# Group averages of channel statistics: a TensorE product against VectorE's 32-partition turns

## The reference

```python
# x (64, 256, 28, 28) f32; M (256, 256, 3, 3); Z (8, 256, 256, 3, 3); alpha (256, 1, 1); rv (1, 8)
def _gn(v, G=32, eps=1e-5):
    g = v.reshape(B_, G, C_ // G, H_, W_)
    m = jnp.mean(g, axis=(2, 3, 4), keepdims=True)
    s = jnp.var(g, axis=(2, 3, 4), keepdims=True)
    return ((g - m) / jnp.sqrt(s + eps)).reshape(v.shape)

A = m * m + jnp.sum(z * z, axis=0) / 100.0
w = (rv @ (z * lax.rsqrt(A)))[0] + m * lax.rsqrt(A)
out = conv3x3(jnp.sign(_gn(x)), jnp.sign(w), padding=1) * alpha
return x + out
```

## Time and profile before

| | us |
|---|---|
| median of 3 runs | 524.27 (523.59 to 525.61) |
| the profiled execution, its own time | 522.31 |
| its span (first to last instruction) | 520.5 |
| HBM read and written | 72.62 MB and 51.38 MB, 238 GB/s over the span |

### The profile page before, as it was taken

How to read it: one execution, slowest core, us unless ns; L and a number is a source line. 1 busy time by engine, 2 the same in 40 slices (tenths; PEclk the granted TensorE clock), 3 DMA queues, 4 the chain that set the end, 5 groups by cost and what they waited for, 6 DMA issues and landing times.

```text
span 520.5 us, 8289 instructions
## 1 busy us (share of the span) xinstructions
PE 482.7 (93%) x2794; PEld 401.2 (77%) x2794; DVE 375.4 (72%) x711; ACT 328.8 (63%) x566; POOL 22.8 (4%) x70
## 2 busy tenths in 40 slices
PE   0898969899999999999999999999999999999990
PEld 0454637788888888888888888888888888888880
DVE  1122458757977978878879879879779779776656
ACT  0787766577667667676676676676676766754320
POOL 8200000000000000000000000000000000000000
PEclk9999997989999999999999999999999999999996
DMA  6999958018568578568568568568577577544226
GB/s 235 399 396 396 397 216 345 0 63 309 214 220 307 191 243 276 211 243 290 191 242 287 195 241 295 191 241 292 197 251 273 210 261 268 202 148 186 87 100 247
DMA packets 45644, 124.37 MB, mean 239 GB/s; under 512 B 3632, under 2 KB 3632, under 8 KB 45616
## 3 DMA queue, kind: packets, MB, share of 16 engines
q1 hardware_dynamic: 45616, 124.01, 65.8%
HBM read 72.62 MB, written 51.38 MB: 238 GB/s over the span
## 4 chain that ended last, share of the span: by engine, by line
PE 86%; DVE 4%; DMA 3%; ACT 2%; SPq 2%; issue 2%; DVEq 0%; ACTq 0%
PE conv_ps L353 80%; DMA m_sb<-in_L_conv_M_dram 3%; SPq L245 2%; PE conv_ps L294 2%; ACT whole L409 1%; DVE x_sb L699 1%; PE conv_ps L307 1%; DVE bn L623 1%; PE conv_ps L297 1%; PE conv_ps L311 1%; PE grp_ps L337 1%; DVE low L605 0%; ACT signs L459 0%; DVE whole L673 0%; ACT low L414 0%
## 5 line engine op out<-in xcount | busy, mean ns | idle before, releaser
L353 PE MATMUL conv_ps<-signs,wts 128*128 128x492 f32 (+5 forms) x1926 | 425.5, 381 | 2.4 <-ACT signs L459 2.1
L353 PEld LDWEIGHTS conv_ps<-signs,wts 128*128 128x128 f32 x1926 | 361.6, 190 | 59.0 <-ACT signs L459 2.5
L467 ACT ACTIVATE part<-conv_ps 128x492 int32<-128x492 f32 (+3 forms) x107 | 61.4, 574 | 147.0 <-PE conv_ps L353 147.0
L459 ACT ACTIVATE signs<-x_sb,shift,rstd 128x784 fp32r<-128x784 f32 x128 | 125.8, 1035 | 0.8 <-DVE shift L660 0.8
L673 DVE SCALAR_TENSOR_TENSOR whole<-conv_ps,part 128x492 int32<-128x492 f32 (+3 forms) x107 | 70.9, 663 | 73.5 <-PE conv_ps L353 65.2
L681 DVE SCALAR_TENSOR_TENSOR low<-whole,conv_ps 128x492 f32<-128x492 int16 (+3 forms) x107 | 70.5, 659 | 3.7
L699 DVE SCALAR_TENSOR_TENSOR x_sb<-whole,alpha_sb,x_sb 128x784 f32<-128x784 int16 x64 | 66.0, 1031 | 0.7
L699 DVE SCALAR_TENSOR_TENSOR x_sb<-low,alpha_sb,x_sb 128x784 f32<-128x784 f32 x64 | 65.9, 1029 | 0.0
L642 DVE BATCH_NORM_STATS2 bn<-x_sb 128x6 f32<-128x392 f32 x116 | 59.7, 557 | 0.8 <-issue 0.6
L437 ACT ACTIVATE unread<-x_sb 128x784 bf16<-128x784 f32 x58 | 49.2, 848 | 0.0
L439 ACT ACTIVATE unread<-x_sb 128x784 bf16<-128x784 f32 x58 | 49.1, 847 | 0.0
(11 more groups left out here) (46 smaller groups left out, 150.5 us busy)
## 6 DMA issues: line engine op xcount, KB each, us to landing
x_sb<-in_x_dram SPq DMA_DIRECT2D x64, 784.0 KB, 5.7
out_dram<-x_sb SPq DMA_DIRECT2D x64, 784.0 KB, 3.8
x_sb<-in_L_conv_Z_dram SPq DMA_DIRECT2D x64, 288.0 KB, 7.4
m_sb<-in_L_conv_M_dram SPq DMA_DIRECT2D x8, 288.0 KB, 8.3
alpha_sb<-in_L_conv_alpha_dram SPq DMA_DIRECT2D x2, 0.5 KB, 2.4
rv_sb<-in_L_conv_rv_dram SPq DMA_DIRECT2D x1, 4.0 KB, 2.4
```

The costliest lines, as they stand in the source:

```text
L353: mm = pe.matmul(sums_of_tile(b, skip, drop), wts[:, ch, kh * KW + kw], e, start=n == 0, stop=n == PRODUCTS - 1, skip_group_check=True)
L459: nc.scalar.activation(o, x_sb[:, slot_of(t, j), h].rearrange("p (a b) -> p a b", b=W), ACT.Sign, bias=shift[:, t % BODY, j, h:h + 1], sca ...
L467: nc.scalar.activation(part[:, bank(b), 0:columns(b)], conv_ps[bank(b)][:, 0:columns(b)], ACT.Copy, scale=-FRACTION / PACK, bias=FRACTION ...
```

## The change

The matrix average, its PSUM bank grp_ps, the TensorE product of each group and ScalarE's copy of it go. VectorE makes the averages with four operations for each group: it turns the blocks of 32 partitions of chan over (32 columns now, of which the first 4 * images hold numbers, so that a partition holds one number and a column one channel), sums runs of CPG columns, multiplies by 1 / CPG, and turns the result back, each average read CPG times, into grp. Each of the four waits for the one before. chan and grp grow to 32 columns, and GpSimd sets chan to zero once in place of building the matrix. GpSimd's variance waits for the turn back.

In the list of VectorE the turn stands ahead of everything else of b = 0, the sum and the scaling behind everything of b = 0, and the turn back ahead of b = 1, in every triple, the first included. In the weight phase, group 0's turn stands behind sums_of_both(0), its other three operations one unit later behind unit_w, and all four of group 1 between copy_taps(3) and copy_taps(5).

```diff
-        average = sb("average", [P, P], F32)
...
-        chan = sb("chan", [P, BODY, TRI, 4], F32)
-        grp = sb("grp", [P, BODY, TRI, 4], F32)
+        chan = sb("chan", [P, BODY, BLOCK // 4, 4], F32)
+        grp = sb("grp", [P, BODY + 1, BLOCK // 4, 4], F32)
+        by_value = sb("by_value", [P, 2, BLOCK], F32)
+        group_sum = sb("group_sum", [P, 2, BLOCK // CPG], F32)
+        group_mean = sb("group_mean", [P, 2, BLOCK // CPG], F32)
...
-        grp_ps = psum("grp_ps", [P, 512], F32)
...
-            def group(g, t, j0, j1, images):
-
-                need(pe, act_sums_done, (images - EARLY) * 2)
-                pe.wait_ge(dve_sums_done, images)
-                need(pe, grp_copied, g)
-                pe.matmul(grp_ps[:, 0:4 * (j1 - j0)], average[:],
-                          chan[:, t % BODY, j0:j1].rearrange("p j k -> p (j k)"), start=True,
-                          stop=True).then_inc(grp_done, 1)
...
-                if c == UNITS - 4:
-                    group(0, 0, 0, 1, 1)
             unit_a(UNITS - 1)
             pack_taps(1)
-            group(1, 0, 1, TRI, TRI)
...
                         first_products(k, t, b, min(b + 1, TRI), number)
-                        if b == (3 if first and t == 0 else 0) and width(t + 1, last) > 0:
-                            group(k + 2, t + 1, 0, width(t + 1, last), k * TRI + TRI + width(t + 1, last))
...
-            def copy_group(g, t, j0, j1):
-                act.wait_ge(grp_done, g + 1)
-                nc.scalar.activation(grp[:, t % BODY, j0:j1].rearrange("p j k -> p (j k)"),
-                                     grp_ps[:, 0:4 * (j1 - j0)], ACT.Copy).then_inc(grp_copied, 1)
...
-                if c == UNITS - 3:
-                    copy_group(0, 0, 0, 1)
...
-            copy_group(1, 0, 1, TRI)
...
-                        if b == (3 if start else 0):
-                            copy_group(k + 2, t + 1, 0, then)
...
+            after(nc.gpsimd.memset(chan[:], 0.0))
...
-                pool.wait_ge(grp_copied, g + 1)
+                pool.wait_ge(grp_done, g + 1)
...
+            def group_turn(g, t, images):
+
+                need(dve, act_sums_done, (images - EARLY) * 2)
+                dve.wait_ge(dve_sums_done, images)
+                nc.vector.transpose(by_value[:, t % 2], chan[:, t % BODY].rearrange("p j k -> p (j k)")
+                                    ).then_inc(grp_step, 1)
+
+            def group_add(g, t):
+
+                dve.wait_ge(grp_step, g * 3 + 1)
+                nc.vector.reduce_sum(group_sum[:, t % 2], by_value[:, t % 2].rearrange("p (g c) -> p g c", c=CPG),
+                                     axis=mybir.AxisListType.X).then_inc(grp_step, 1)
+
+            def group_scale(g, t):
+
+                dve.wait_ge(grp_step, g * 3 + 2)
+                nc.vector.tensor_scalar(group_mean[:, t % 2], group_sum[:, t % 2], 1.0 / CPG, None,
+                                        ALU.mult).then_inc(grp_step, 1)
+
+            def group_back(g, t, spot=None):
+
+                spot = t % BODY if spot is None else spot
+                dve.wait_ge(grp_step, g * 3 + 3)
+                nc.vector.transpose(grp[:, spot].rearrange("p (g c) k -> p g (c k)", c=CPG // 4),
+                                    group_mean[:, t % 2].unsqueeze(2).to_broadcast([P, BLOCK // CPG, CPG])
+                                    ).then_inc(grp_done, 1)
...
                 if c == UNITS - 5:
                     sums_of_both(0)
+                    group_turn(0, 0, 1)
+                if c == UNITS - 4:
+                    group_add(0, 0)
+                    group_scale(0, 0)
+                    group_back(0, 0, BODY)
...
             copy_taps(3)
+            group_turn(1, 0, TRI)
+            group_add(1, 0)
+            group_scale(1, 0)
+            group_back(1, 0)
             copy_taps(5)
...
                     for b in range(TILES):
+                        if b == 0:
+                            group_turn(k + 2, t + 1, k * TRI + TRI + then)
+                        if b == 1:
+                            group_back(k + 2, t + 1)
                         if b >= 2 and b - 2 < later and b > 2:
...
                         if not start and 1 <= b < 1 + TRI:
                             outputs(t - 1, b - 1, end)
+                        if b == 0:
+                            group_add(k + 2, t + 1)
+                            group_scale(k + 2, t + 1)
```

More of the change, by code:

```diff
@@ L68, in conv_preact @@
     CPG = C // GROUPS
+    BLOCK = 32
+    assert BLOCK % CPG == 0 and TRI * 4 <= BLOCK
     INV_LAG = 2
@@ L74, in conv_preact @@
     KQ = P // QUAD
-    CONST_STEPS = 2 * 4 + 3 + 3 + 1 + KQ
+    CONST_STEPS = 2 * 4 + 3 + 1 + 1 + KQ
     Z_DMAS = 16 * (K // KQ * KQ + 1)
@@ L164, in conv_preact @@
         bn_step = sem("bn_step")
+        grp_step = sem("grp_step")
         grp_done = sem("grp_done")
-        grp_copied = sem("grp_copied")
         var_step = sem("var_step")
@@ L549, in _, with variance @@
                                               base=0, pattern=[[-1, P]], channel_multiplier=1))
[L550 to L556, removed]
+            after(nc.gpsimd.memset(chan[:], 0.0))
             nc.gpsimd.memset(signs[:].bitcast(F32), 0.0).then_inc(borders_zero, 1)
-            def variance(g, t, j0, j1):
-                pool.wait_ge(grp_copied, g + 1)
+            def variance(g, t, j0, j1, spot=None):
+                pool.wait_ge(grp_done, g + 1)
                 v = slice(j0, j1)
-                mean = grp[:, t % BODY, v, 0:4:2]
+                spot = t % BODY if spot is None else spot
+                mean = grp[:, spot, v, 0:4:2]
                 nc.gpsimd.tensor_tensor(mean_sq[:, t % BODY, v], mean, mean, ALU.mult).then_inc(var_step, 1)
                 pool.wait_ge(var_step, g * 2 + 1)
-                nc.gpsimd.tensor_tensor(var[:, t % BODY, v], grp[:, t % BODY, v, 1:4:2], mean_sq[:, t % BODY, v],
+                nc.gpsimd.tensor_tensor(var[:, t % BODY, v], grp[:, spot, v, 1:4:2], mean_sq[:, t % BODY, v],
                                         ALU.subtract).then_inc(var_step, 1)
-            variance(0, 0, 0, 1)
+            variance(0, 0, 0, 1, BODY)
             variance(1, 0, 1, TRI)
@@ L655, in bounded, with negative_mean @@
                                         ALU.add).then_inc(var_done, 1)
-            def negative_mean(g, t, j0, j1):
+            def group_turn(g, t, images):
[12 more added lines that the diff above has]
+            def group_back(g, t, spot=None):
+                spot = t % BODY if spot is None else spot
+                dve.wait_ge(grp_step, g * 3 + 3)
+                nc.vector.transpose(grp[:, spot].rearrange("p (g c) k -> p g (c k)", c=CPG // 4),
+                                    group_mean[:, t % 2].unsqueeze(2).to_broadcast([P, BLOCK // CPG, CPG])
+                                    ).then_inc(grp_done, 1)
+            def negative_mean(g, t, j0, j1, spot=None):
+                spot = t % BODY if spot is None else spot
                 dve.wait_ge(rstd_done, g + 1)
-                nc.vector.scalar_tensor_tensor(out=shift[:, t % BODY, j0:j1], in0=grp[:, t % BODY, j0:j1, 0:4:2],
+                nc.vector.scalar_tensor_tensor(out=shift[:, t % BODY, j0:j1], in0=grp[:, spot, j0:j1, 0:4:2],
                                                scalar=-1.0, in1=rstd[:, t % BODY, j0:j1], op0=ALU.mult,
@@ L709, in _ @@
                     sums_of_both(0)
+                    group_turn(0, 0, 1)
[3 more added lines that the diff above has]
+                    group_back(0, 0, BODY)
                 if c == UNITS - 2:
                     bounded(0, 0, 0, 1)
-                    negative_mean(0, 0, 0, 1)
+                    negative_mean(0, 0, 0, 1, BODY)
             unit_w(UNITS - 2)
```

## The result

| | before | changed |
|---|---|---|
| median of 6 runs, us | 524.36 (522.71 to 525.61) | 518.30 (517.04 to 519.63) |
| span of the profiled execution | 520.5 | 515.3 |
| step of a triple (90 products) | 19.79 | 19.57 |
| VectorE busy in a triple | 16.47 | 17.10 |

The ratio is 0.9887, 95% interval 0.9861 to 0.9913, so 4.6 to 7.3 us less, 5.9 in the middle. The forecast was 4.7 us less, 519.6 us.

A forecast was written before the change was run, and what follows sets the result against it. TensorE was taken to bound the kernel in the triples. Removing 21 group products gives -4.9 us, group 0 in the weight phase +0.25, so -4.7: 524.27 to 519.6 us, range 517.5 to 522.4.

The forecast's parts named there:

- The bound: In the triples TensorE alone bounds the kernel, busy all 19.80 us of one, with VectorE at 16.47 and ScalarE at 13.55.
- The price of a group, 0.235 us: On TensorE, the same pair of products with and without a group between: 0.65 against 0.42 us, unrounded 0.235.
- the chain's 0.12: Rival price of a group on TensorE: only 0.12 us for each of 21, time 522.0 us; chance 0.10 including a second variant.
- 21 groups: Of 23 groups 21 lie in the triples, all on the path, first triple included: 21 x 0.235 = 4.9 us less.
- The four operations, 0.91 us: Added to VectorE per group: three at 0.25 and one at 0.16 us, 1.07 us with waits; bounds 0.64 and 3.0.
- The cover in the triples: VectorE's added 1.07 us fits into 3.33 us of idle time per triple, slips have 10 us; price nothing.
- rival C: Every triple: VectorE becomes the bound from 3.33 us a group; at 4.1 us, 16 us more, 540; chance 0.05.
- Group 0, +0.25 us: Weight phase: the turn ahead of m_sq delays the path by 0.25 us, from 0.16 to 0.6 by the bounds.
- Group 1, hidden in 1.33 us: Weight phase: the four operations, 1.07 us, fit into VectorE's 1.33 us idle ahead of copy_taps(5), costing nothing.
- The first triple: VectorE reads the first tile up to 1 us later, covered by 10 us; TensorE's 2.07 us pause before 103.66 stays.
- The sum: Whole kernel: -4.9 + 0.25 = -4.7 us, from 524.27 to 519.6 us; forecast's chance 0.72.
- Rival B: TensorE's clock: one half-rate stretch more or fewer moves the time by 1.4 us, to 521.0 or 518.2; chance 0.09.

The follow-up runs named there:

- twice: The kernel before with each group's TensorE product issued twice, the second into columns nobody reads; ratio 1.0131 to before, step 20.02 us.
- one_pass: The kernel before with the group product in bf16 in place of f32; 521.66 us, ratio 0.9965, step 19.70 us.
- after_third: The changed kernel, unchanged, measured a third time; 519.07 us, ratio 0.9895 to before, step 19.57 us.
- bare: The changed kernel without the four VectorE operations of each group, statistics read per channel; 518.67 us, ratio 0.9897 to before, step 19.57 us.
- load3: The changed kernel with three more VectorE operations in each triple, each writing 512 columns nobody reads; ratio 0.9908, step 19.57 us.
- load7: The changed kernel with seven more VectorE operations in each triple, each writing 512 columns nobody reads; 571.7 us, ratio 1.0919.
- after_again: The changed kernel, unchanged, measured a second time; 518.94 us, ratio 0.9901 to before, step 19.57 us.

## Why the prediction was right, and where it wasn't

**The bound.** Right. TensorE is one piece from the second triple to the end, before and after.

**The price of a group, 0.235 us.** Nearly right: the step fell by 0.22. The prediction says that 0.235 comes from the unrounded starts, but those give 0.228 (0.651 less 0.423). The 0.01 that is still missing goes on the products behind, which run a little slower where no group stood in front. The choice between the chain's 0.12 and the pair's 0.23 decided the forecast, and twice and one_pass show why the chain's figure was no price. The rule that the prediction weighed, from the Trainium skill ("TensorE: Matmul & The Clock Gate", section "Step-by-step: what each phase is for"), that weight loads are pulled ahead and run beside the product in front, fits the group's first load, which starts with the product in front at 266.51. It doesn't fit the one behind the group, 0.08 us late, nor the price of 0.05 us that the prediction made of it with the floor: 0.22 measured, and 0.13 with a single bf16 pass.

**21 groups.** Right: 20 steps of 0.22 are 4.4 us (from the second triple's first product to the start of the last of all it is 404.64 us before and 400.27 in after_third, both with the stretch, which makes 4.37), and the group of the first triple, with the time at half rate taken at half, 0.2 to 0.3.

**The four operations, 0.91 us.** 0.77 measured (211, 180, 170 and 212 ns), inside the bounds: 0.18 to 0.21 where the row with 32 columns gave 0.25, 0.17 where 0.16 was taken. VectorE's busy time in a triple rose by only 0.63, since an operation that waits for nothing starts inside the tail of the turn in front of it (260.87 behind 260.74 + 0.21).

**The cover in the triples.** Right: 0.77 us and another three operations of 0.485 us cost nothing (bare, load3). Past it rival C is worse than the sum of busy times made it, as load7 shows (53 us where the sum gives 43): the wait of the turn is not empty when VectorE is late.

**Group 0, +0.25 us.** Wrong, the term of the sum that was mis-sized: measured 0.0 (24.40, 24.37 and 24.39 us). The pause of 0.16 us stood in the earlier trace rows itself and the turn went into it. The first product did start 0.28 us later (81.29), which seemed to bear the forecast out, but the weights had landed that much later in that execution (49.42 and 49.11).

**Group 1, hidden in 1.33 us.** Right: the wait before copy_taps(5) is 0.54 us now, 0.79 less.

**The first triple.** Right: the pause of 2.07 us stayed.

**The sum.** The change is worth 4.4 + 0.25 = 4.6 to 4.7 us, by the steps, the first triple's group and bare. 4.7 was forecast, with two misses of 0.25 to 0.3 us that cancel, so that the figure is as good as it is by luck. The comparison gave 5.9 and the two later ones 5.2 and 5.5; 4.7 lies inside all three intervals, near the lower edge of the first and the third.

**Rival B.** It had a part in the two first profiles: the stretch behind the first triple was in that of before and not in the changed one, and made 1.57 of their 5.2 us. (The prediction priced it at 1.4 from a window that cuts its start off.) That it also fills the gap in the medians isn't borne out. Span times (1 - mean granted clock) is what an execution lost to the half rate. On one chip that was 9.5 us before (17 executions) and 9.8 for the changed kernel (5, after_again), on the other 10.6 (11) and 10.2 (6, after_third): 0.3 more here and 0.4 less there, with either kernel spread over a few us. Nor does the kernel before always meet the stretch: in 9 of 55 executions of before its mean clock was 0.986, above every profile that has the stretch (0.983 at most). So no effect of the change on the clock is shown, and what the medians show beyond 4.7 us may be chance.

## What to carry to other kernels

Price a small matmul in a dense stream by the distance between its neighbours with and without it, at another place of the same trace. Here that gave 0.23 us where the chain charged 0.12. Before you count on an idle share of an engine as cover, ask in which order its list waits: most of the idle time was free here, but past it a wait at the head of the list tied three engines together and came on top of the overrun. And compare phases, not absolute starts, between two executions: a start that moves by 0.3 us may be a load that landed later, and one that moves by 1.5 a stretch at half rate.

## What the runs showed of the hardware

- VectorE turns 128 x 32 f32 (blocks of 32 partitions) in 0.21 us, also when the source is read eight times over; a sum over runs of 8 in 32 columns takes 0.18 us, setting 512 columns of f32 0.485 us.
- Behind a short TensorE product the next one needs 0.09 us more to the following start, with f32 (0.305) as with bf16 (0.305, against 0.216 without), and the weight load in between starts 0.08 us late. The two f32 passes of 12 columns start 0.03 us apart (266.72 and 266.75).
- Behind a pause of 2.07 us in a dense stream TensorE's clock fell to the 1.2 GHz level for 3.4 us in 6 of 9 profiles, with one and the same program in one execution and not in another; it costs 1.57 us.
- A stretch of the same length at 50 us, behind a wait for weights, showed in 7 of 13 profiles and put off the first product of the triples by 1.3 to 1.6 us.
